# The first four units of a batched gate kernel in another order: T2 ahead of T3, B22's products ahead of T2's, quarters scaled on other engines

## The reference

```python
q_emb = relu(cond @ W3 + b3)                       # one row of 1024 for each entry
v_sum = sum(x, axis=tokens)
out   = x + relu((n * x + v_sum) * q_emb @ W2 + b2)  # n = 128, W2 is 1024 x 1024, all in fp32
```

## Time and profile before

| | |
|---|---|
| median of 3 runs | 650.03 us (649.55 to 651.1) |
| the profiled execution | 652.42 us, its span 650.3 us |
| busy share of the span | TensorE 97%, VectorE 69%, ScalarE 63%, GpSimd 6% |
| matmuls of the 225 products | 2700 |
| GpSimd's last work | 73 us |
| mean granted TensorE clock | 0.987 |

### The profile page before, as it was taken

One profiled execution on the slowest core, in us unless ns is written; L12 is line 12 of the kernel. 1 busy time (PEld: TensorE's weight loads), 2 busy tenths in 40 slices (PEclk: granted clock), 3 DMA queues, 4 the chain that ended last, 5 costly groups with the idle time before them and its releaser, 6 DMA issues.

```text
span 650.3 us, 9176 instructions
## 1 busy us (share of the span) xinstructions
PE 631.9 (97%) x2779; PEld 519.1 (80%) x2779; DVE 445.7 (69%) x692; ACT 411.4 (63%) x878; POOL 39.8 (6%) x52
## 2 busy tenths in 40 slices
PE   9996798999999999999999999999999999999997
PEld 6784676888888888888888888888888888888886
DVE  4886858867576776767677675768667576876633
ACT  4765367775939577593956749485674948668320
POOL 2677100000000000000000000000000000000000
PEclk9997988999999999999999999999999999999999
DMA  8996434736343353734336363433636433360603
GB/s 328 407 272 171 91 130 194 256 135 244 144 170 123 156 197 129 251 136 152 130 162 200 129 233 154 146 122 160 217 129 233 154 130 133 161 223 1 231 27 129
DMA packets 27951, 111.98 MB, mean 172 GB/s; under 512 B 3104, under 2 KB 3744, under 8 KB 24352
## 3 DMA queue, kind: packets, MB, share of 16 engines
q1 hardware_dynamic: 26352, 107.36, 45.9%
q0 software_dynamic: 1152, 4.19, 3.4%
q10 hardware_dynamic: 432, 0.27, 0.2%
HBM read 78.25 MB, written 33.55 MB: 172 GB/s over the span
## 4 chain that ended last, share of the span: by engine, by line
PE 87%; POOL 3%; DVE 3%; DMA 2%; ACT 2%; issue 2%; SPq 0%; DVEq 0%; ACTq 0%; POOLq 0%
PE acc L354 87%; POOL x_sb L721 2%; DMA w_stage<-w_q 1%; ACT x_sb L502 1%; DMA x_sb<-x_t 1%; DVE w_lo L877 1%; DVE vsum L766 1%; DVE a_lo L844 0%; ACT a_hi L488 0%; ACT w_hi L529 0%; POOL w_stage L727 0%; SPq L231 0%; DVE xn L882 0%; POOL b_step L748 0%; POOL x_sb L733 0%
## 5 line engine op out<-in xcount | busy, mean ns | idle before, releaser
L354 PE MATMUL acc<-w_hi,a_hi 128*128 128x512 f32 x900 | 353.6, 393 | 13.8 <-issue 10.0
L354 PE MATMUL acc<-w_lo,a_hi 128*128 128x512 f32 x900 | 352.1, 391 | 0.0
L354 PE MATMUL acc<-w_hi,a_lo 128*128 128x512 f32 x900 | 352.1, 391 | 0.0
L354 PEld LDWEIGHTS acc<-w_hi,a_hi 128*128 128x128 f32 x900 | 170.2, 189 | 52.4 <-issue 12.2
L502 ACT ACTIVATE x_sb<-x_sb,bias,scale 128x128 f32<-128x128 f32 x468 | 193.3, 486 | 22.6 <-DVE bias L772 22.6
L354 PEld LDWEIGHTS acc<-w_hi,a_lo 128*128 128x128 f32 x900 | 170.1, 189 | 35.8
L354 PEld LDWEIGHTS acc<-w_lo,a_hi 128*128 128x128 f32 x900 | 170.4, 189 | 35.1
L872 DVE TENSOR_TENSOR a_lo<-x_sb,a_hi 128x512 fp32r<-128x512 f32 x140 | 96.7, 690 | 105.9 <-ACT a_hi L497 105.4
L497 ACT CAST a_hi<-x_sb 128x512 fp32r<-128x512 f32 x140 | 87.1, 622 | 37.6 <-PE acc L354 36.1
L766 DVE TENSOR_REDUCE vsum<-x_sb 128x16 f32<-128x2048 f32 (+2 forms) x43 | 74.4, 1733 | 10.9 <-DMA x_sb<-x_t 10.9
L497 ACT CAST a_hi<-s 128x512 fp32r<-128x512 f32 x56 | 34.8, 622 | 72.8 <-PE acc L354 69.1
(11 more groups left out here) (59 smaller groups left out, 241.1 us busy)
## 6 DMA issues: line engine op xcount, KB each, us to landing
xn<-x SPq DMA_DIRECT2D x64, 512.0 KB, 4.0
out<-xn SPq DMA_DIRECT2D x62, 512.0 KB, 3.0
x_sb<-x_t SPq DMA_DIRECT2D x28, 1024.0 KB, 4.9
x_sb<-x_t SPq DMA_DIRECT2D x7, 512.0 KB, 11.4
w_stage<-w_q POOLq DMA_DIRECT2D x6, 512.0 KB, 7.7
xn<-w_t SPq DMA_DIRECT2D x4, 512.0 KB, 6.5
u_sb<-w_q SPq DMA_DIRECT2D x2, 512.0 KB, 9.7
m_sb<-w_q SPq DMA_DIRECT2D x2, 512.0 KB, 9.4
```

The lines of the kernel that those rows point to most:

```text
L354: return nc.tensor.matmul(dst, lhs, rhs, start=False, stop=False, skip_group_check=True)
```

## The change

- `LATE` has another order: m = 3 of units 1, 2, 3 (B22) directly behind m = 5, then m = 6 (T2), m = 7 (T3) and m = 4 (T4). T2 is cast ahead of T3.
- T1's two additions are issued when the low parts of B21's halves are made, ahead of all GpSimd work on units 1 to 3 (before: behind the scaling of A12 of unit 2).
- Quarters scaled elsewhere: (unit 2, A12) on VectorE, (3, A11) and (1, A21) on ScalarE (all GpSimd before); of (0, A21) one tile goes from GpSimd to VectorE, of (0, A22) two tiles from GpSimd to ScalarE. S3 of unit 1 is made by VectorE. GpSimd keeps seven stretches in a new order; S3 of unit 2 comes behind T2's additions.
- The token sums of (2, A12) and (2, A22), and of (3, A11) and (3, A21), are taken in one instruction each.
- `load_next(1)` comes ahead of the first store of unit 1.
- ScalarE's and VectorE's queues are rewritten for this order.

The diff, cut to its core:

```diff
-    LATE = [(1, 5), (2, 5), (3, 5), (1, 3), (1, 6), (2, 3), (1, 7), (3, 3), (2, 6), (3, 6), (1, 4),
+    LATE = [(1, 5), (2, 5), (3, 5), (1, 3), (2, 3), (3, 3), (1, 6), (2, 6), (1, 7), (3, 6), (1, 4),
             (2, 7), (3, 7), (2, 4), (3, 4)]
-             (1, A21), (1, A22), (3, A12), (2, A21), (2, A22), (3, A21)]
-    BOTH = (3, A12)
+             (1, A21), (1, A22), (3, A12), (2, A21)]
+    BOTH = [(2, A12), (3, A11), (3, A12)]
...
@@ sync
-            store_first(1, 0, (c11_done, c12_done))
             sp.wait_ge(lo_ready, late(1, 4) + 1)
             load_next(1)
+            store_first(1, 0, (c11_done, c12_done))
...
@@ scalar
             cast_first(4)
+            scale_second_half(0, A22)
             cast_first(5)
-            seed_q_u1()
             scale_first(1, A12)
             cast_first(6)
+            seed_q_u1()
+            cast_w("b12", 0, b12_loaded[0])
             cast_first(7)
             seed_q(1, 1, 0)
-            for h in range(2):
-                cast_w("b12", h, b12_loaded[h])
+            cast_w("b12", 1, b12_loaded[1])
...
+            scale_first(3, A11)
             cast_first(8)
             for h in range(2):
                 cast_w("b22", h, b22_loaded[h])
+            scale_first(2, A22)
...
             for h in range(2):
                 cast_w("t1", h, t1_summed[h])
+            scale_first(1, A21)
             scale_first(3, A12)
             cast_first(9)
+            seed_q(1, 1, 1)
+            cast_first(late(1, 5))
             scale_first(3, A22)
-            seed_q(1, 1, 1)
-            scale_first(2, A22)
-            cast_first(late(1, 5))
-            for h in range(2):
-                cast_w("t3", h, t3_summed[h])
             act.wait_ge(b_step_ready, 1)
             act.wait_ge(c12_done, 1)
             nc.scalar.copy(acc[:, U1_BANK[5]], b_step[:]).then_inc(r_u1_seeded, 1)
+            cast_first(late(2, 5))
             act.wait_ge(c21_done, 1)
             nc.scalar.copy(r_bank(0), b_step[:]).then_inc(r_seeded, 1)
-            cast_first(late(2, 5))
-            cast_w("t2", 0, t2_summed[0])
+            cast_first(late(3, 5))
...
             cast_first(late(1, 3))
-            cast_first(late(1, 6))
+            cast_w("t2", 0, t2_summed[0])
             save_m5(1, 0)
             cast_first(late(2, 3))
+            cast_w("t2", 1, t2_summed[1])
             save_m5(1, 1)
+            cast_first(late(3, 3))
+            cast_first(late(1, 6))
+            cast_first(late(2, 6))
+            for h in range(2):
+                cast_w("t3", h, t3_summed[h])
+            scale_usual(2, 0, 0)
             cast_first(late(1, 7))
-            scale_usual(2, 0, 0)
-            cast_first(late(3, 3))
+            cast_first(late(3, 6))
+            cast_first(late(1, 4))
+            cast_first(late(2, 7))
+            cast_w("t4", 0, t4_summed[0])
             save_u2_u1()
...
+            cast_first(late(2, 4))
             scale_usual(2, 0, 1)
-            cast_first(late(2, 7))
+            cast_first(late(3, 4))
             scale_usual(2, 0, 2)
...
             save_u2(1, 1, 0)
-            scale_usual(2, 0, 3)
             save_u2(1, 1, 1)
-            for n in (4, 5):
+            for n in (3, 4, 5):
                 scale_usual(2, 0, n)
...
@@ gpsimd
             scale_tiles(0, A11, range(2, KH))
-            scale_tiles(0, A21, range(KH // 2))
+            scale_tiles(0, A21, range(1))
             scale_tiles(0, A12, range(KH))
-            scale_tiles(0, A22, range(KH))
-            scale_tiles(2, A12, range(KH))
-            pool.wait_ge(w_lo_ready, split("b21", 1))
-            for h in range(2):
+            scale_tiles(0, A22, range(KH // 2))
+            for h in range(2):
+                pool.wait_ge(w_lo_ready, split("b21", h))
                 add_half(w_halves, 0, 1, h, t1_summed)
-            scale_tiles(3, A11, range(KH))
+            scale_tiles(3, A21, range(KH))
+            pool.wait_ge(b_seeded, len(SEEDED))
+            nc.gpsimd.tensor_tensor(b_step[:], b_step[:], b_first[:], ALU.add).then_inc(b_step_ready, 1)
+            scale_tiles(1, A22, range(KH))
             for h in range(2):
                 pool.wait_ge(w_lo_ready, split("b12", h))
                 add_half(v_halves, 1, 1, h, t3_summed)
-            pool.wait_ge(b_seeded, len(SEEDED))
-            nc.gpsimd.tensor_tensor(b_step[:], b_step[:], b_first[:], ALU.add).then_inc(b_step_ready, 1)
-            scale_tiles(1, A21, range(KH))
-            s3(1)
-            scale_tiles(1, A22, range(KH))
+            s3(3)
+            scale_tiles(2, A21, range(KH))
             for h in range(2):
                 pool.wait_ge(w_lo_ready, split("t1", h))
                 add_half(w_halves, 1, 1, h, t2_summed)
-            scale_tiles(2, A21, range(KH))
             s3(2)
-            scale_tiles(3, A21, range(KH))
-            s3(3)
...
@@ vector
+            scale_tiles(u, A21, range(1, 2), 2).then_inc(x0_scaled[0, A21], 1)
...
+            stats(1, A12)
             low_w("b21", 0)
-            stats(1, A12)
             low_first(4)
             low_w("b21", 1)
+            low_first(5)
             stats(2, A12)
-            low_first(5)
+            low_first(6)
+            scale_tiles(2, A12, range(KH), stat(2, A12)).then_inc(x0_scaled[2, A12], 1)
             stats(3, A11)
...
             first_result(1, 2, 1, 0, 0, c11_done)
-            for h in range(2):
-                low_w("t1", h)
+            s3_u1()
+            sum_first(1, 5)
             stats(2, A21)
             low_first(9)
-            sum_first(1, 5)
+            low_first(late(1, 5))
             first_result(0, "c12", 0, 0, 1, c12_done)
-            stats(2, A22)
-            low_first(late(1, 5))
+            sum_first(2, 5)
             first_result(0, "c21", 0, 1, 0, c21_done)
-            stats(3, A21)
-            sum_first(2, 5)
+            low_first(late(2, 5))
             first_result(0, "c22", 0, 1, 1, c22_done)
-            low_first(late(2, 5))
             sum_first(3, 5)
             sum_first(1, 6)
             low_first(late(3, 5))
             sum_first(1, 3)
-            low_w("t3", 0)
+            sum_first(2, 6)
             low_first(late(1, 3))
...
+            low_w("t4", 0)
+            c12_u1()
             low_first(late(3, 7))
+            low_w("t4", 1)
+            low_first(late(2, 4))
+            c22_u1()
+            low_first(late(3, 4))
             sums_usual(0, 1, x_loaded[1], 16)
             scalars_usual(2, 0, 1)
-            low_first(late(2, 4))
-            low_first(late(3, 4))
             c11(1, 0)
```

More of the change, by code:

```diff
@@ L64, in cond_residual, with stat @@
     STATS = [(0, A11), (0, A21), (1, A11), (2, A11), (0, A12), (0, A22), (1, A12), (2, A12), (3, A11),
-             (1, A21), (1, A22), (3, A12), (2, A21), (2, A22), (3, A21)]
-    BOTH = (3, A12)
-    SPLIT = [("b11", 4), ("b21", 2), ("b12", 2), ("b22", 2), ("t1", 2), ("t3", 2), ("t2", 2), ("t4", 2)]
+             (1, A21), (1, A22), (3, A12), (2, A21)]
+    BOTH = [(2, A12), (3, A11), (3, A12)]
+    def stat(u, q):
+        return STATS.index((u, q) if (u, q) in STATS else (u, (0, q[1]))) + 1
+    SPLIT = [("b11", 4), ("b21", 2), ("b12", 2), ("b22", 2), ("t1", 2), ("t2", 2), ("t3", 2), ("t4", 2)]
     W_PLACE = {"b11": W_SLOT[1], "b21": W_SLOT[2], "b12": W_SLOT[4], "t1": W_SLOT[5], "b22": W_SLOT[3],
@@ L144, in cond_residual @@
         t4_summed = [sem(f"t4_summed{h}") for h in range(2)]
-        s3_ready = sem("s3_ready")
+        s3_ready = {u: sem(f"s3_ready{u}") for u in (1, 2, 3)}
         q_u1_seeded, r_u1_seeded = sem("q_u1_seeded"), sem("r_u1_seeded")
@@ L474, in cast_first @@
                 if o < EARLY:
-                    act.wait_ge(x0_scaled[u, q], 2 if o == 1 else 1)
+                    act.wait_ge(x0_scaled[u, q], {1: 3, 5: 2}.get(o, 1))
                 else:
@@ L480, in cast_first @@
                     elif m == 7:
-                        act.wait_ge(s3_ready, u)
+                        act.wait_ge(s3_ready[u], 1)
                     else:
@@ L506, in scale_first @@
             def scale_first(u, q):
-                act.wait_ge(scalars_first, STATS.index((u, A12 if (u, q) == (3, A22) else q)) + 1)
+                act.wait_ge(scalars_first, stat(u, q))
                 scale_quarter(u, q, x0_scaled[u, q])
@@ L732, in s3 @@
                 pool.wait_ge(x0_scaled[u, A21], 1)
-                nc.gpsimd.tensor_tensor(quarter(u, A11), quarter(u, A11), quarter(u, A21), ALU.subtract).then_inc(s3_ready, 1)
+                nc.gpsimd.tensor_tensor(quarter(u, A11), quarter(u, A11), quarter(u, A21), ALU.subtract).then_inc(s3_ready[u], 1)
             scale_tiles(0, A11, range(2, KH))
-            scale_tiles(0, A21, range(KH // 2))
+            scale_tiles(0, A21, range(1))
             scale_tiles(0, A12, range(KH))
-            scale_tiles(0, A22, range(KH))
-            scale_tiles(2, A12, range(KH))
-            pool.wait_ge(w_lo_ready, split("b21", 1))
+            scale_tiles(0, A22, range(KH // 2))
```

(61 more changed lines are left out.)

20 lines of the change are left out of this document (6 added, 14 removed).

## The result

The changed kernel takes 635.24 us (median of 4 runs, 634.93 to 636.66) against 650.42 for the one before, measured beside it: ratio 0.9772, 95% interval 0.9752 to 0.9791, so 15.2 us less. The profiled execution took 635.19 us with a span of 633.4, 16.9 less than the span of before; that execution of the kernel before lay 2 us above its median. The forecast was 634.5.

The account below looks back on a forecast made before the run. TensorE bounds the steady part, so only the opening gives: product 29 16.6 us earlier, 15.6 after allowances. Profiled 652.42 less 15.6 is 636.8, less 2.4 to the median 634.5 us; own range 633 to 637, with other cases 630.8 to 641.5.

Parts of the forecast that it names:

- The bound: TensorE bounds the steady part; only the opening, up to product 29, can give, at most 22.9 us.
- Up to product 14: Product 13 starts at 49.9 and product 14 at 52.6 instead of 59.47: 6.9 us, plus 1.6 of low clock.
- The anchor: S3 of unit 2 on GpSimd ends at 52.8; VectorE's sum (2, 5) waits for it; product 15 has margin 0.4.
- the allowance: 0.7 us, half of 1.4, for GpSimd working beside VectorE's `stats` twice ahead of S3 of unit 2.
- The chain behind it: VectorE runs without pause from 52.8 to 83.2, 30.4 us, then operands to 90.0; the 4.47 us wait goes.
- The wait at product 27: TensorE wants product 27's operand at 88.0 and gets it at 90.0: 2.0 us of wait stay, as 1.97 before.
- the 1.7 us of low clock: Behind product 27's wait TensorE runs at its lower clock, costing 1.7 us (bounds nothing and 2.2).
- the sum with allowances: Product 29 at 97.1, 16.6 us earlier; allowances of 0.7 for meetings and 0.3 for near ties leave 15.6.
- All of it goes: Rival: product 27's wait or its low clock also vanishes, 1.7 to 3.7 us more: 630.8 to 632.8; chance 0.15.
- The slip of the anchor: Rival: T1's second half lands at 45.0, S3 of unit 2 ends at 55.6; with low clock 4.4 us, 638.9; chance 0.25.
- its last case: The late T1 landing with a GpSimd quarter at 6.17 us beside it: 641.5; chance 0.25 for the whole rival.
- the lock rule: On the port VectorE and GpSimd share, the second blocks for a whole instruction; ahead of S3, 1.3 us more lost.

Follow-up runs that it names:

- the two kernels with moved copies: Kernel before with save_u2_u1's copy moved ahead of unit 4's scaling, alone (646.29 us) or with product 14's bias copy ahead of T3's casts (647.15 us).
- both copies moved: Kernel before with product 14's bias copy ahead of T3's casts and save_u2_u1's copy ahead of unit 4's scaling on ScalarE: 647.15 us.
- T3 in the hole: Kernel after with T3's casts and low parts put in the idle time of ScalarE and VectorE ahead of sum (2, 5): 637.15 us.

## Why the prediction was right, point by point

- **The bound** was read rightly: only the opening could give, and what follows product 29 took 536.6 us in every kernel.
- **Up to product 14** held to 0.1 us, with T1's second half at 37.7. Its loads of B22 came later than I had it, by 5.3 us (33.0 to 38.4) and not 3 to 4, so the casts didn't quite cover it: ScalarE stood 2.1 us for them and cast T1 at 41.4, where I had 40.5.
- **The anchor** held as a mechanism: VectorE stands 3.95 us for S3, and moving S3 or T1 moves product 27 by nearly as much. Its time was 1.1 us late against 52.8, 0.4 beyond the allowance. GpSimd's three terms together were right, 5.6 us for 5.9 (48.31 to 53.9; 46.8 to 52.8 with the handover); they began 1.5 late. Of that, 0.9 is there when T1's low parts start (43.1 for 42.2). Two things lie ahead of them: VectorE stood for GpSimd twice (1.33 us for 0.17 and 0.91 for 0.16; the 0.7 was for this), and ScalarE cast T1 late behind B22's loads. Which had the larger part, no run separates. The other 0.6 is VectorE's work from there to 48.2, which has no pause and which I had too short.
- **The chain behind it**: from sum (2, 5) to `c22_sum` 36.5 us were measured and 36.5 forecast (52.8 to 89.3, which is 90.0 less the 0.7 of `c22_sum`). The terms of its first part add to 30.2 and not to the 30.4 that I wrote; measured were 30.5, to 84.4.
- **The wait at product 27** was there with 1.62 for 2.0; the 1.7 us of low clock that I took with it was not. This term failed, and as it is larger than the anchor's slip, product 29 came 0.3 us ahead of 97.1 and 1.3 ahead of the sum with allowances. That 97.1 fits to 0.3 is luck: a term too large against a start too late.
- **The median.** The profile gained 16.9 us where the sum said 15.6, the medians 15.2. The profiled execution of before was 2.4 above its median and the one of after is on it. All executions profiled have the same 536.6 us behind product 29, so the 2.4 sat in waits of the opening (1.6 of it shows ahead of product 14), and the change takes those away. So taking 2.4 off the 636.8 was wrong: the new kernel should have been forecast at 636.8, and it measured 635.2, the 1.6 less being mostly the low clock that stayed away. These two errors cancelled in the 634.5, and that it lies within 0.8 of the median is in part luck.
- **The rivals.** "All of it goes" named what happened at product 27 as its second case, the low clock that vanishes, at 632.8. The clock did; the time did not come, by the two points above. The slip of the anchor was priced rightly at 2.8 (2.9 measured) and its low clock wrongly; its last case adds to 641.7, where 641.5 is written. For the meetings of VectorE and GpSimd I kept 0.7 and put 1.3 more on the lock rule, 2.0 in all: in the kernel after VectorE stood 1.9 us in two of them ahead of the anchor, nearer to the rule, and in other kernels single meetings held it up by 1.9 to 2.8.
- **Where the gain comes from.** T1's early issue 2.4, the two quarters on ScalarE 3.4, the order of unit 5's load 4.4, each by undoing it alone. These don't add up to shares, since a low clock goes with the last. The place of T2's product, undone, cost 2.0, of which 1.0 at most is its own. What B22's products ahead of T2's, S3 of unit 1 on VectorE and the merged sums are worth was not tried alone.

## What to carry to other kernels

Where several in-order queues feed one engine, don't price the stop that the timeline shows, but the first late item behind which the queues run without a pause: removing two visible stops gave 4 us, moving the chain gave 15. An idle stretch of an engine isn't free room if the work put there and the work it waits for exclude each other, as VectorE's low parts and GpSimd's S3 did here. And look for a result that stands behind an unrelated wait in program order: one moved line was worth 2 us here.

## What was not expected of the hardware

- **VectorE stood for GpSimd's whole instruction, even for tiny work.** In the kernel after the bias of (1, A22), four columns, took 1.33 us and ended with GpSimd's addition, and a `scale` of eight columns took 0.91 and ended with GpSimd's S3 of unit 3. VectorE's timeline, then GpSimd's:

```profile
35.48 1.33 DVE L774 TENSOR_TENSOR bias<-vsum,q_emb 128x4 f32<-128x4 f32 x1
...
42.23 0.91 DVE L772 TENSOR_SCALAR scale<-q_emb 128x8 f32<-128x8 f32 x1
```

```profile
35.49 1.29 POOL L750 TENSOR_TENSOR b_step<-b_step,b_first 128x512 f32<-128x512 f32 x1
```

  Low parts of 1.2 us took 3.1 and 3.3, a sum of 0.7 took 3.5. The Trainium skill (SBUF — State Buffer, SBUF: two separate sides) puts a VectorE instruction with two SBUF inputs under the lock against a GpSimd instruction that reads SBUF; the rows of the bias, the low parts and the sum agree.
- **The low clock doesn't go by the length of the wait alone.** It came behind waits of 1.89 us (product 13 with quarters back on GpSimd), 1.97, 2.45 and 2.47 (product 26 in the two kernels with moved copies) and 3.9 us or more, and not behind 1.64 or less, 1.98 and 2.22 (products 21 and 14 with both copies moved) or 2.69 us (T3 in the hole).
- **Landings of GpSimd's additions vary.** T2's second half, issued at about 51 us, landed 8.2 to 10.4 us later (59.3 to 62.1) in seven profiles that have the same work up to there or nearly so.
